# Product keys with a split fused matrix and the sequence kept in DRAM; experts' weights turned by DVE

## The reference

```
xn  = batch_norm(inputs)                                  # over all 2048 tokens, per feature
q   = (xn @ w_q.T) in 2 axes x 8 heads x 128
sim = einsum('pbnhd,hkpd->pbnhk', q, keys)                # 64 keys per axis and head
best 8 per axis -> 64 sums -> best 8: scores, idx
o   = einsum('bnd,bnhkd->bnhk', inputs, key_in[idx])
o   = gelu(o) * softmax(scores)
out = einsum('bnhk,bnhkd->bnd', o, key_out[idx])
```

```
hg, hu = x @ w_gate[e].T, x @ w_up[e].T                    # 256 x 256 each
y     += combine[:, e] * ((silu(hg) * hu) @ w_down[e].T)
y     += (silu(x @ shared_gate.T) * (x @ shared_up.T)) @ shared_down.T
```

## Time and profile before

| what | value |
|---|---|
| median of 3 executions | 2093.97 us (2093.91 to 2094.64) |
| the profiled execution's own time | 2091.08 us |
| its span | 2089.4 us |
| mean granted TensorE clock | 0.952 |
| TensorE busy | 1887.6 us (90%) |
| TensorE weight loads | 1562.4 us (75%, beside the matmuls) |
| DVE busy | 1317.8 us (63%) |
| ScalarE busy | 658.2 us (32%) |
| GpSimd busy | 159.5 us (8%) |

### The profile page before, as it was taken

How to read it: one execution, slowest core, us unless ns; L and a number is a source line. 1 busy time by engine, 2 the same in 40 slices (tenths; PEclk the granted TensorE clock), 3 DMA queues, 4 the chain that set the end, 5 groups by cost and what they waited for, 6 DMA issues and landing times. The chain is left out here.

```text
span 2089.4 us, 43354 instructions
## 1 busy us (share of the span) xinstructions
PE 1887.6 (90%) x16947; PEld 1562.4 (75%) x16947; DVE 1317.8 (63%) x3525; ACT 658.2 (32%) x1491; POOL 159.5 (8%) x118
## 2 busy tenths in 40 slices
PE   6999998799459999999999858869899999999998
PEld 5877886576348887887788735557788888888887
DVE  4555555377558888888888546655655555555554
ACT  3444344244122312321231124525323232332332
POOL 0000000110100000000000054631000000000000
PEclk9999999799559999999999879989999999999999
DMA  4000000000730000000000030001100010000001
GB/s 153 1 0 0 0 1 1 11 16 10 149 63 2 1 1 0 1 1 1 0 1 1 2 99 1 0 1 36 31 16 31 15 30 15 26 19 16 30 15 41
DMA packets 43212, 43.73 MB, mean 21 GB/s; under 512 B 3906, under 2 KB 42338, under 8 KB 43106
## 3 DMA queue, kind: packets, MB, share of 16 engines
q1 hardware_dynamic: 43106, 42.44, 7.7%
HBM read 40.34 MB, written 2.10 MB: 20 GB/s over the span
## 5 line engine op out<-in xcount | busy, mean ns | idle before, releaser
L2208 PE MATMUL f_out<-f_ko,f_gel 128*128 128x256 f32 x1024 | 238.3, 393 | 15.5 <-DVE f_gel L2377 14.7
L2208 PEld LDWEIGHTS f_out<-f_ko,f_gel 128*128 128x128 f32 x1024 | 198.8, 197 | 45.6 <-DVE f_gel L2377 14.2
L2645 DVE TENSOR_TENSOR m_act_up<-m_silu,m_up 128x512 f32<-128x512 f32 x136 | 93.6, 688 | 212.9 <-PE m_up L586 207.0
L2572 ACT ACTIVATE m_silu<-m_gate 128x512 f32<-128x512 f32 x136 | 81.4, 598 | 270.7 <-PE m_gate L586 270.7
L2631 DVE SCALAR_TENSOR_TENSOR g_x<-m_y,m_combine,g_x 128x256 f32<-128x256 f32 x272 | 118.9, 479 | 51.7 <-PE m_y L586 50.2
L232 ACT ACTIVATE a_prob<-a_score,a_neg_max 128x128 f32<-128x128 f32 x256 | 90.5, 365 | 170.2 <-DVE a_neg_max L222 170.2
L586 PE MATMUL f_act<-f_hT_pair_high,f_kiT_high 128*128 128x256 f32 x384 | 123.4, 321 | 0.3 <-ACT f_gel L2253 0.3
L2253 ACT ACTIVATE f_gel<-f_act 128x512 f32<-128x512 f32 x128 | 75.4, 597 | 126.0 <-PE f_act L586 107.5
L586 PE MATMUL f_act<-f_hT_pair_low,f_kiT_high 128*128 128x256 f32 x384 | 108.1, 282 | 0.0
L586 PE MATMUL f_act<-f_hT_pair_high,f_kiT_low 128*128 128x256 f32 x384 | 107.9, 281 | 0.0
L2637 DVE TENSOR_TENSOR m_hidden_low<-m_act_up,m_hidden_high 128x512 fp32r<-128x512 f32 x136 | 93.3, 686 | 1.5
(11 more groups left out here) (373 smaller groups left out, 4878.2 us busy)
## 6 DMA issues: line engine op xcount, KB each, us to landing
f_gel<-in_L_ffn_key_in SPq DMA_DIRECT2D x2, 2048.0 KB, 21.6
f_ko<-in_L_ffn_key_out SPq DMA_DIRECT2D x2, 2048.0 KB, 33.5
g_experts_w<-in_L_ffn_w_gate SPq DMA_DIRECT2D x16, 256.0 KB, 2.7
g_experts_w<-in_L_ffn_w_up SPq DMA_DIRECT2D x16, 256.0 KB, 3.0
g_experts_w<-in_L_ffn_w_down SPq DMA_DIRECT2D x16, 256.0 KB, 3.6
m_chunked_ctx<-in_ctx SPq DMA_DIRECT2D x8, 256.0 KB, 2.7
fp_wq_nat<-in_L_ffn_w_q SPq DMA_DIRECT2D x1, 2048.0 KB, 10.3
g_ctx_next<-in_ctx SPq DMA_DIRECT2D x8, 256.0 KB, 2.7
```

The costliest lines, as they stand in the source:

```text
L2208: last = pe.matmul(out_bank[:, t, :], gel[:, r, t * P:(t + 1) * P], ko[:, r, :], start=(r == 0), stop=(r == R - 1))
L2572: act.activation(silu[:, m, :], gate_bank[m][:, :], ACT.Silu).then_inc(silu_ready[m].sem, 1)
L2645: dve.tensor_tensor(act_up[:, m, :], silu[:, m, :], up_bank[m][:, :], ALU.mult) \
```

## The change

In the product keys, `hT` lives in the preparation block alone. SP stores it to DRAM (`h_kept`) at the end of that block, and the main block loads one pair of it at a time into `h_pair`, the next pair after the fourth activation step. The fused matrix and the batch-normed pair are held in high and low parts, so that a similarity step is three fp32r matmuls in place of one float32; the parts take a copy on ScalarE and a subtraction on DVE, for the matrix once and for every pair. The activations start with the blocks that stayed float32 (24 to 31) and end with block 23. The next pair's first similarities move from behind the weight groups into the first half's output sum, ahead of blocks 24 to 27.

In the experts, a matrix of the next expert is loaded as 32 x 32 squares: 24 DMAs of 32 KB for each expert, in pieces of 128 bytes, into two buffers in turn, the first expert's at the end of the late loads. DVE turns each square with one transpose instruction a matrix into `w_turn` in SBUF, at the head of the token groups 0, 1 and 2, and ScalarE and DVE make high and low part from there. TensorE's `turn_weights` and its PSUM bank go away.

```diff
+    def load_blocks(self, sp, dst, weights, loaded):
+
+        n = self.BLOCK
+        for m, w in enumerate(weights):
+            blocks = w.rearrange("e (a i) (k b j) -> (e i) b k a j", i=n, k=KD, j=n)
+            for b in range(P // n):
+                for k in range(KD):
+                    sp.dma_start(dst[n * b:n * (b + 1), m, k, :].rearrange("i (a j) -> i a j", j=n), blocks[:, b, k, :, :]) \
+                        .then_inc(loaded, 16)
...
+        self.load_blocks(sp, self.first_blocks, self.first, self.blocks_loaded)
...
-        hT = s.sb("hT", [P, KD, TOKENS])
+        h_kept = nc.dram_tensor("h_kept", (P, KD, TOKENS), F32, kind="Internal").ap()
-        fused = s.sb("fused", [P, KD, 2 * H * NK])
+        fused = [s.sb(f"fused_{part}", [P, KD, 2 * H * NK], F32R) for part in ("high", "low")]
...
+                sp.wait_ge(pair_copied, PAIRS)
+                sp.dma_start(h_kept, hT[:, :, :]).then_inc(h_stored, 16)
+                sp.wait_ge(h_stored, 16)
...
-                copy_fused(act, act.copy, 0)
+                for n in range(4):
+                    act.wait_ge(fused_ready[n % 2], n // 2 + 1)
+                    act.copy(fused_part(fused[0], n), banks[n % 2][:, :]).then_inc(fused_high, 1)
...
-                copy_fused(dve, dve.tensor_copy, 1)
+                for n in range(4):
+                    dve.wait_ge(fused_high, n + 1)
+                    dve.tensor_tensor(fused_part(fused[1], n), banks[n % 2][:, :], fused_part(fused[0], n), ALU.subtract) \
+                        .then_inc(fused_copied[n % 2], 1)
...
+        @block.sync
+        def _(sp):
+            sp.dma_start(h_pair[:, :, :], h_kept[:, :, 0:2 * P]).then_inc(h_loaded, 16)
+            with sp.Fori(1, PAIRS) as n:
+                sp.wait_ge(act_ready[1], 8 * n - 6)
+                sp.dma_start(h_pair[:, :, :], h_kept[:, :, bass.ds(n * 2 * P, 2 * P)]).then_inc(h_loaded, 16)
...
+            act.wait_ge(h_loaded, 16 * n + 16)
...
+            act.copy(xb_pair[0][:, :, :], xb[:, :, :]).then_inc(xb_high, 1)
+            act.copy(hT_pair[0][:, :, :], h_pair[:, :, :]).then_inc(h_high, 1)
+
+        def rows_of(step):
+
+            return 2 * ((step + SPLIT // 2) % (R // 2))
...
-                last = pe.matmul(sim_bank[ax][:, :], xbT[:, k, t * P:(t + 1) * P],
-                                 fused[:, k, ax * 512:(ax + 1) * 512], start=(k == 0), stop=(k == KD - 1))
+                last = split_product(pe, sim_bank[ax][:, :], [part[:, k, t * P:(t + 1) * P] for part in xb_pair],
+                                     [part[:, k, ax * 512:(ax + 1) * 512] for part in fused], k == 0, k == KD - 1)
...
+                    if 24 <= r < 28:
+                        similarities(i + 1, 0, r - 24)
...
-                    similarities(i + 1, 0, m)
...
+                    dve.wait_ge(xb_high, i + 1)
+                    dve.tensor_tensor(xb_pair[1][:, :, :], xb[:, :, :], xb_pair[0][:, :, :], ALU.subtract).then_inc(xb_low, 1)
...
+            load_blocks(2, 0)
+            with sp.Fori(1, NE // 2) as h:
+                for n in (1, 0):
+                    e = 2 * h + 2 - n
+                    wait(sp, w_turned, e - 2, 3)
+                    load_blocks(e, n)
...
-        def turn_weights(pe, e, m):
...
-                if g < 3 and not last_one:
-                    turn_weights(pe, e + 1, g)
...
-                act.copy(wT[par][0][:, m, :, :].rearrange("p k n -> p (k n)"), turn_bank[:, :]).then_inc(w_high.sem, 1)
+                act.copy(wT[par][0][:, m, :, :], w_turn[:, m, :, :]).then_inc(w_high.sem, 1)
...
+            def turn_blocks(e, par, m):
+                if m == 0:
+                    dve.wait_ge(w_loaded[par], (LOADED // 2) * (e + par))
+                dve.transpose(w_turn[:, m, :, :].rearrange("p k n -> p (k n)"),
+                              w_blocks[par][:, m, :, :].rearrange("p k n -> p (k n)")).then_inc(w_turned.sem, 1)
...
                 for g in range(GROUPS):
+                    if g < 3 and not last_one:
+                        turn_blocks(e + 1, 1 - par, g)
```

More of the change, by code:

```diff
@@ L1551, with __init__ @@
     HID = 256
-    def __init__(self, s, ctx_in, w_in, b_in, gate_w, gate_b, s_gate, s_up, s_down):
+    BLOCK = 32
+    LOADED = 16 * 3 * KD * (P // BLOCK)
+    def __init__(self, s, ctx_in, w_in, b_in, gate_w, gate_b, s_gate, s_up, s_down, w_gate, w_up, w_down):
         self.ctx_in, self.w_in, self.b_in, self.gate_w, self.gate_b = ctx_in, w_in, b_in, gate_w, gate_b
         self.shared = (s_gate, s_up, s_down)
+        self.first = [w[0:1, :, :] for w in (w_gate, w_up, w_down)]
+        self.first_blocks = s.sb("first_blocks", [P, 3, KD, self.HID])
+        self.blocks_loaded = s.sem("late_blocks_loaded")
         self.w_nat = s.sb("aligned_w", [P, 2, D])
@@ L2016, in _, with fused_part @@
                 turner.wait_all(pe)
[L2018 to L2022, removed]
+            def fused_part(part, n):
+                return part[:, n // 2, (n % 2) * H * NK:(n % 2 + 1) * H * NK]
             @block.scalar
@@ L2061, in _ @@
                 turner.split_on_dve(dve)
-        xbT = s.sb("xbT", [P, KD, 2 * P])
+        h_pair = s.sb("h_pair", [P, KD, 2 * P])
+        xb = s.sb("xb", [P, KD, 2 * P])
+        xb_pair = [s.sb(f"xb_pair_{part}", [P, KD, 2 * P], F32R) for part in ("high", "low")]
         hT_pair = [s.sb(f"hT_pair_{part}", [P, KD, 2 * P], F32R) for part in ("high", "low")]
@@ L2174, in activations @@
                             else:
[L2175 removed]
+                                last = pe.matmul(dst, kiT_rest[:, k, r - SPLIT, :], h_pair[:, k, :],
                                                  start=(k == 0), stop=(k == KD - 1))
@@ L2425, in stage_experts @@
     TAKEN = -3.0e38
+    LOADED = late.LOADED
     with ExitStack() as ctx:
         s = Scope(nc, ctx, "m")
-        gate_bias, xnT, route_bank, w_nat = late.gate_bias, late.xnT, late.route_bank, late.experts_w
+        gate_bias, xnT, route_bank = late.gate_bias, late.xnT, late.route_bank
+        w_blocks = [s.sb("w_blocks", [P, 3, KD, HID]), late.first_blocks]
+        w_turn = s.sb("w_turn", [P, 3, KD, HID])
         score = s.sb("score", [P, NB, NE])
@@ L2446, in stage_experts @@
         logits_exp = s.sem("logits_exp")
-        w_loaded = s.sem("w_loaded")
+        w_loaded = [s.sem("w_loaded"), late.blocks_loaded]
         w_turned = s.counting("w_turned", 3)
@@ L2469, in _, with load_blocks @@
                 sp.sem_inc(done.sem, 3)
-            with sp.Fori(1, NE + 1) as e:
-                wait(sp, w_turned, e, 0)
-                for m, w in enumerate((w_gate, w_up, w_down)):
-                    sp.dma_start(w_nat[:, 2 * m:2 * m + 2, :],
-                                 w[bass.ds(e - 1, 1), :, :].rearrange("a o n -> (a o) n").rearrange("(t p) n -> p t n", p=P)) \
-                        .then_inc(w_loaded, 16)
-            sp.wait_ge(w_loaded, 48 * NE)
+            def load_blocks(e, n):
+                late.load_blocks(sp, w_blocks[n], [w[bass.ds(e - 1, 1), :, :] for w in (w_gate, w_up, w_down)], w_loaded[n])
+            load_blocks(2, 0)
[4 more added lines that the diff above has]
+                    load_blocks(e, n)
+            for n in range(2):
+                sp.wait_ge(w_loaded[n], LOADED * NE // 2)
             tiles = out.rearrange("b t d -> t b d")
@@ L2496, in all_experts @@
             on_engine(NE, 0, last_one=True)
-        def turn_weights(pe, e, m):
-            pe.wait_ge(w_loaded, 48 * e)
-            wait(pe, w_low, e, m)
-            for k in range(KD):
-                for t in range(2):
-                    last = pe.transpose(turn_bank[:, k * HID + t * P:k * HID + (t + 1) * P],
-                                        w_nat[:, 2 * m + t, k * P:(k + 1) * P], ident[:, :])
-            last.then_inc(w_turned.sem, 1)
         def expert_on_pe(pe, e, par, last_one=False):
@@ L2588, in copy_weights @@
                 wait(dve, w_high, e, m + 1)
-                high, low = (w[:, m, :, :].rearrange("p k n -> p (k n)") for w in wT[par])
-                dve.tensor_tensor(low, turn_bank[:, :], high, ALU.subtract).then_inc(w_low.sem, 1)
+                high, low = (w[:, m, :, :] for w in wT[par])
+                dve.tensor_tensor(low, w_turn[:, m, :, :], high, ALU.subtract).then_inc(w_low.sem, 1)
+            def turn_blocks(e, par, m):
[3 more added lines that the diff above has]
+                              w_blocks[par][:, m, :, :].rearrange("p k n -> p (k n)")).then_inc(w_turned.sem, 1)
             route_links.link(dve, dve.tensor_copy(score[:, :, :], route_bank[:, :, 0, :]))
```

26 lines of the change are left out of this document (16 added, 10 removed).

## The result

The changed kernel takes 2107.31 us (median of 5 executions, 2103.09 to 2110.95) against 2093.97 of the kernel before: a ratio of 1.0056 with a 95% interval of 1.0044 to 1.0067, so it is slower, by 13.3 us between the medians. The profiled execution has a span of 2102.9 us, 13.5 more. TensorE is busy 1871.8 us, 15.8 less than before, so it waits more.

A forecast was written before the change was run, and what follows sets the result against it. TensorE was taken to bound the experts, and DVE the end of the product keys' weight stretch. Experts -20.5, pairs +30.0 and start +4.4 gave +13.9 us, 2107.9 us on the median; range 2086 to 2120.

The forecast's parts named there:

- The experts' 20.5 us: Experts: 48 turns of four transposes, 0.455 us each, leave TensorE; expert 0 credited with nothing; 20.5 us saved.
- DVE's turning: Experts: one DVE turning a matrix takes 0.69 us, hidden before the group's first product.
- The rival's 1.03 us of cover: Experts: a DVE turning beyond 1.03 us delays products, at most 17 us, 2125 in all; chance 0.07.
- The squares: Experts: 24 loads take up to 20 us, hidden within 33.9 us an expert; late-squares rival +74 us, chance 0.06.
- The pair's order: Product keys: moving similarities into the first output sum adds 2.73 us and returns 1.45, net +1.28 a pair.
- The clock: Product keys: emptied stretch slows TensorE's clock, 3.0 us a pair in the first sum, seven pairs; rival, clock holds: 0.17.
- 4.2 us of slow clock: Product keys: upper bound of the slow clock's price in each of seven pairs, given as 2118 us in all.
- The start: Product keys' start: loading the first pair, making its parts and waits delay the first similarity; +4.4 us in sum.
- the attention stages' 2.45 us: Gated and aligned attention, between product keys and experts: the forecast had no change there, 0.

The follow-up runs named there:

- experiment 8: The changed kernel with every DVE transpose of the experts' squares done a second time into an unread buffer: 2105.98 us, ratio 1.0061 to the kernel before.
- experiment 9: The changed kernel with every square loaded a second time into an unread buffer: 2107.37 us, ratio 1.0068 to the kernel before.
- experiment 1: The kernel before with only the experts' part of the change: 2076.83 us, ratio 0.9926.
- experiment 3: The changed kernel with 18 unread matmuls a pair between activations and first output sum, in the first seven pairs: 2095.62 us, ratio 1.0005 to the kernel before.
- experiment 4: The changed kernel with unread matmuls before the first output sum and seven more before every second one: 2085.49 us, ratio 0.9958 to the kernel before.
- experiment 7: The kernel before with the experts' part, seven unread matmuls before every second output sum and four behind each weight group of the last pair: 2068.66 us, ratio 0.9885.
- experiment 5: The changed kernel with the similarities back behind the third and fourth weight groups and DVE's subtraction moved up: 2092.28 us, ratio 0.9994 to the kernel before.
- experiment 2: The kernel before with only the product keys' part of the change: 2127.73 us, ratio 1.0153.
- experiment 6: The changed kernel with similarities back among the weight groups and TensorE's waits filled with unread matmuls: 2077.44 us, ratio 0.9933 to the kernel before.

## Why the prediction was right, step by step

**The experts' 20.5 us: right.** 15 experts got 1.33 us shorter each (35.39 to 34.06 on the mean), where 3 x 0.455 = 1.37 were forecast, and expert 0 gained nothing, as was credited (37.01 and 37.09). The rest of the 1.2 us missing is the end, 0.55 us longer; it is so with the product keys' part alone too (41.00 us, 40.51 in the kernel before and 41.06 in the changed one), so it is no price of the new turning.

**DVE's turning: right.** 0.70 us against 0.69 from the nearest row, hidden, and by experiment 8 hidden twice over. The rival's 1.03 us of cover was the wrong limit: two turnings end 1.3 us after the first one's start and cost nothing, since there is slack behind the product as well.

**The squares: right, with the reason too careful.** SP's issue sets the pace, 11.7 us a load where 20 were allowed. The Trainium skill (DMA: Bandwidth & Descriptors, the anatomy of a DMA) gives about 2.0 us of fixed cost, for DMAs that GpSimd issues; SP's landed in 1.9 us here, close to it. But 24 of them one after another would be 46 us, and experiment 9 issues 48 in 23.6 us and hides them.

**The pair's order: right.** Forecast were -0.70 before T, -0.75 in the stretch and +2.73 in the sum, net +1.28; measured are -0.82, -0.89 and +2.79, net +1.08.

**The clock: right in mechanism, two terms mis-sized, the sum right by luck.** The forecast put 3.0 us a pair into the first sum, taken from the last pair. It lost 1.68 there on the mean (1.4 to 2.3). Even the last pair's 3.0 was the price of one execution: in experiment 1 the same instructions took 11.99 us, 1.4 over 10.60. The second sum, which the forecast left out, lost 1.09 (14.70 us on the mean before, 15.79 after). That it is the clock, and that empty TensorE time brings it down, experiments 3, 4 and 7 show: added work removes each loss where it is added. The two errors nearly cancel, for no reason that the forecast gave: with 1.08 for the order and 0.2 at the turn from pair to pair that is 4.03 a pair, 28.2 for seven, where 30.0 were forecast. Why the second sum was slow in half the pairs before and in all after, behind the same wait of 1.82 us, stays open. One bound was also added up wrongly: 4.2 us of slow clock in each of seven pairs gives 2116 us by the forecast's own terms, not 2118.

**The start: too high in sum, too low in its parts.** From the main block's start to the first similarity the load, the parts and the waits cost 5.3 us, where 2.7 + 0.55 + 0.69 + 0.1 = 4.0 were forecast. That only 3.2 us were left at the first similarity is because the block began 2.1 us earlier, behind a preparation at a higher clock, which was not forecast. At the end of the first activations 1.45 were left; the pair's own -0.82 counts there too, and the clock rose at another moment.

**Not foreseen: the attention stages' 2.45 us.** With the product keys' part alone, which changes nothing in those stages, they took 5.1 us more. Over the traces their time goes with the granted clock of the stretch: 277.3 us at 0.91 (experiment 8), 278.1 at 0.90 (before), 280.4 to 281.1 at 0.89 (the changed kernel, experiments 3 to 5), 281.3 at 0.88 (experiment 7), 283.2 to 283.8 at 0.87 (experiments 1, 2 and 9). Only experiment 6, 283.5 at 0.89, stands apart. Why the clock differs there from run to run is not shown.

## What to carry to other kernels

Work that seems to cost TensorE time while it waits for another engine may be what holds its clock; before moving it, look at what stays in the stretch, and at a place in the same trace where the stretch already runs without it. A handful of matmuls that nobody reads, in a bank that is free, replaces it, at no cost where they fit the wait: 25 of them a pair took the changed kernel from 2107 to 2085 us here, and 7 a pair, with 16 more in the last, the experts' part from 2077 to 2069. Moving transposes from the full engine to a half-idle one was worth what the seam in the timeline said, 1.33 us an expert where three times 0.455 were read. And a price taken from one place of one trace is one sample: look for the same instructions in a second trace before it goes into a sum.

## What the runs showed of the hardware

- The same wait of 1.82 us ahead of the same 64 matmuls was followed by 14.05 us or by 15.4 to 15.7 within one execution of the kernel before (15.4 to 17.1 in the changed one). With the wait filled, all were 14.05, and the four executions of experiment 7 lay within 2.3 us of each other, where the six of experiment 1 lay within 12.5.
- DVE turned 128 x 512 float32 numbers in 32 x 32 squares in 0.70 us, 0.63 apart.
- Loads of 32 KB in 128-byte pieces were issued 0.49 us apart and landed in 1.9 us, 48 of them no slower than 24.
